# Four GNN layers on one core: 46 instead of 29 bundles of edges counted in the first layer, and their turned products five tiles later

## The reference, cut to what matters

```python
def setup_inputs(seed=0):
    x   # 6250 x 128, float32
    src = randint(0, 6250)                    # 200000
    dst = (6250 * uniform ** 2.0)             # 200000, then both sorted by dst
    edge_type_8, edge_weight1                 # 8 relations, one weight per edge

def reference(...):
    h = relu(layernorm(x)); x = x + layer1(h, src, dst)   # mean of h[src] over the edges of a node, W, b
    h = relu(layernorm(x)); x = x + layer2(h, src, dst)   # gates:
        theta = h[dst] - h[src]
        w = sigmoid(relu(theta @ W1 + b1) @ W2 + b2)
        agg = segment_sum(w * theta, dst) + indeg * (h @ W4 + b4)
    h = relu(layernorm(x)); x = x + layer3(h, src, dst)   # mean of relu(h @ Wp.T + bp)[src]
    h = relu(layernorm(x)); x = x + layer4(h, src, dst)   # sum over 8 relations, weight per edge
    return x
```

## Time and profile before

| | |
|---|---|
| time, median of 3 runs | 6365.12 us (6364.78 to 6367.93) |
| span of the profiled execution | 6426.8 us |
| layer 1, edges | 107 to 1233 us |
| layer 2, edges | 1304 to 3642 us |
| layer 3, edges | 3700 to 4320 us |
| layer 4, edges | 4530 to 6426 us |
| busy over the span | PE 60%, DVE 46%, ACT 22%, POOL 62% |
| indirect DMAs | 3505 on GpSimd |
| stores of counts | 29 in layer 1, 19 in layer 2 |

### The profile page before, as it was taken

One profiled execution on the slowest core, in us unless ns is written; L12 is line 12 of the kernel. 1 busy time (PEld: TensorE's weight loads), 2 busy tenths in 40 slices (PEclk: granted clock), 3 DMA queues, 4 the chain that ended last, 5 costly groups with the idle time before them and its releaser, 6 DMA issues.

```text
span 6426.8 us, 68888 instructions
## 1 busy us (share of the span) xinstructions
PE 3872.2 (60%) x20122; PEld 2959.4 (46%) x20154; DVE 2933.5 (46%) x9989; ACT 1413.8 (22%) x5474; POOL 3972.3 (62%) x4198
## 2 busy tenths in 40 slices
PE   4676766655555565555555578876565565665433
PEld 3333434445544454455455456653344444444332
DVE  7555544556555565556555633342333222222222
ACT  4222122333333333333333401121000000000000
POOL 4556666456666666666666466646566666666665
PEclk7778778777777777777777789998777777777666
DMA  3333333345455454544545455555211111111121
GB/s 107 96 101 110 111 105 116 107 140 155 143 150 148 147 150 144 154 145 141 159 144 151 123 184 198 195 181 178 69 46 46 45 47 45 46 45 46 46 61 46
DMA packets 323521, 734.49 MB, mean 114 GB/s; under 512 B 77056, under 2 KB 164124, under 8 KB 310860
## 3 DMA queue, kind: packets, MB, share of 16 engines
q0 software_dynamic: 172432, 405.32, 23.2%
q1 hardware_dynamic: 148700, 323.81, 14.9%
q10 hardware_dynamic: 2016, 0.92, 0.1%
HBM read 598.71 MB, written 131.05 MB: 114 GB/s over the span
## 4 chain that ended last, share of the span: by engine, by line
another core or an unknown queue 30%; PE 27%; DVE 19%; issue 15%; ACT 4%; DMA 2%; DVEq 1%; SPq 1%; ACTq 0%
PE ps L2574 8%; DVE oneh L1863 6%; PE ps L2559 3%; PE ps L2530 3%; PE ps L2537 2%; DVE ps L1998 2%; PE ps L2469 2%; PE ps L2597 2%; DMA third<-dst_flat 2%; ACT turned_words L1681 1%; DVE third L1990 1%; PE ps L2419 1%; DVE turned_words L1955 1%; DVE tmp L1954 1%
## 5 line engine op out<-in xcount | busy, mean ns | idle before, releaser
L1470 POOL DMA_INDIRECT rows<-tab_rel,third x1299 | 1247.0, 960 | 646.9 <-issue 367.1
L1470 POOL DMA_INDIRECT rows<-tab_h,idx_src x1086 | 1046.7, 964 | 723.4 <-issue 345.8
L1470 POOL DMA_INDIRECT rows<-tab_hp,idx_src x1120 | 1077.1, 962 | 622.5 <-issue 298.8
L2597 PE MATMUL ps<-third 128*128 128x128 f32 x3126 | 607.1, 353 | 501.6 <-issue 295.8
L2530 PE MATMUL ps<-oneh,rows 128*128 128x128 f32 x2598 | 489.1, 340 | 607.1 <-DVE oneh L1863 330.7
L2597 PEld LDWEIGHTS ps<-third 128*128 128x128 f32 x3126 | 539.6, 258 | 593.7 <-issue 355.3
L2574 PE MATMUL ps<-third,h 128*120 128x384 bf16 (+17 forms) x3773 | 715.0, 337 | 65.8 <-issue 34.6
L2530 PEld LDWEIGHTS ps<-oneh,rows 128*128 128x128 f32 x2598 | 432.6, 245 | 695.8 <-DVE oneh L1863 362.6
L1681 ACT ACTIVATE turned_words<-turned_words 128x128 f32<-128x128 f32 x1563 | 463.1, 300 | 690.8 <-DVE turned_words L2003 527.5
L2574 PEld LDWEIGHTS ps<-third,h 128*120 128x120 bf16 (+10 forms) x3773 | 487.8, 133 | 239.4 <-issue 61.3
L1470 POOL DMA_INDIRECT third<-tab_hp,idx_src x443 | 425.9, 961 | 231.7 <-issue 118.5
(11 more groups left out here) (279 smaller groups left out, 5495.4 us busy)
## 6 DMA issues: line engine op xcount, KB each, us to landing
third<-dst_flat SPq DMA_DIRECT2D x390, 256.0 KB
h<-cnt_d SPq DMA_DIRECT2D x48, 1568.0 KB
cnt_d<-h SPq DMA_DIRECT2D x29, 1568.0 KB
cnt_d<-third SPq DMA_DIRECT2D x19, 1568.0 KB
tab_rel<-third SPq DMA_DIRECT2D x49, 512.0 KB
rows<-tab_rel,third POOLq DMA_INDIRECT x1299
rows<-tab_hp,idx_src POOLq DMA_INDIRECT x1120
rows<-tab_h,idx_src POOLq DMA_INDIRECT x1086
```

The lines of the kernel that those rows point to most:

```text
L1470: pool.indirect_dma_start(out=to[:, t, 0:n], out_offset=None, in_=table[:, :], in_offset=bass.IndirectOffsetOnAxis(ap=idx[:, col:col + 1], ...
L2597: last = pe.matmul(ps_t[sl][:, t * P:(t + 1) * P], onehT[:, sl, t * P:(t + 1) * P], pwin[:, st["v"] % 2, :], start=True, stop=True)
```

## The change

Three numbers are changed or added. `FIRST_SHARE` goes from 880/1563 to 1160/1563. With it 46 bundles (1148 tiles) are counted in layer 1 and 415 tiles (104 groups) gathered there, and 2 bundles (20 tiles) are left for layer 2. The 17 bundles that move have windows of 14 to 17 columns and 14 to 18 tiles each. `per_turn` of layer 1 goes from 2346.8 to 6205.8 ns, that of layer 2 from 262.7 to 19.7 ns. `LATE_TURN` and `LATE_ADD` put the turned product of a bundle in layer 1 five steps (before one) behind `pack_out`, and the addition three steps (before one) behind the turned product. Layer 3 keeps its steps and its work. Nothing else differs. The changed lines of the constants and of `multiply` move later code down by one and by three lines (L2559 is L2562 after it, L2584 is L2587).

```diff
@@ -25,7 +25,8 @@
 PACK = 2
 PACK_SHARE = 1168 / 1563
 
-FIRST_SHARE = 880 / 1563
+FIRST_SHARE = 1160 / 1563
+LATE_TURN, LATE_ADD = 5, 3
 BUNDLE = 128
 
 PACKS3 = ((4, 36), (2, 76), (1, 148))
@@ -885,10 +886,12 @@
                     plan.append(("pack_mm", dict(st, q0=q0, q1=min(nb, q0 + MULTIPLY_STEP))))
                     yield MULTIPLY_STEP * H3 / 2.4
                 plan.append(("pack_out", st))
-                yield 0.0
+                for _ in range(LATE_TURN if layer == 0 else 1):
+                    yield 0.0
                 st["added"] = n_added.get(u - 1, 0)
                 plan.append(("pack_turn", st))
-                yield 0.0
+                for _ in range(LATE_ADD if layer == 0 else 1):
+                    yield 0.0
                 plan.append(("pack_add", dict(u=u, sums=sums, turn=n_turn[u], add=s_add.value)))
                 n_added[u] = s_add.up()
                 yield 0.0
```

## The result

The changed kernel takes 6218.91 us (median of 4 runs, 6206.78 to 6221.39) against 6366.52 us (6364.78 to 6371.44): a ratio of 0.9767, 95% interval 0.9749 to 0.9785. The forecast was 6307 us. The direction was right and the time lies in the range, but the gain is 148 us where 58 were forecast. And it is a gain only on some chips: the runs further down fell on several chips, of two kinds, and on the second kind, where the kernel before takes 5463 us, the same change makes it 1.5% slower.

The account below looks back on a forecast made before the run. Layer 1 was taken as bound by a chain, not an engine, with TensorE waiting before the turned product. Layer 1 +26 us (610 less 46 x 12.7) and layer 2 -84 gave -58: 6365.1 to 6307 us, 8-in-10 range 6170 to 6520.

Parts of the forecast that it names:

- Seventeen more bundles: Layer 1: 17 more bundles, each costing what a late bundle cost before, 35.9 us: +610 us.
- Fewer gathered groups: Layer 1: 3.7 fewer groups a bundle, 1.3 us of TensorE scatter each: 4.8 us saved a bundle.
- The late turned product: Layer 1: counts fill TensorE's wait before the turned product, 6.9 us saved a bundle, ends 1.7 and 13.8.
- Rival A: End of each layer 1 product: signals stay late, only 8.3 us saved a bundle, 6509 us, slower; chance 0.33.
- The moved addition: Layer 1: covered by the counting, 0.34 us on VectorE needed only 16 tiles later: nothing gained.
- Signals that come sooner: Layer 1 products: fewer groups between steps and a higher clock, 1 us saved a bundle, ends 0 and 16.
- Stores: Layer 1: seventeen stores of 1568 KB move in, DMA share 0.35, SyncE otherwise free there: nothing.
- Layer 2: Layer 2 without 276 late tiles: faster gathers and fewer waits for loads behind stores, -84 us.
- rival C: Layer 2 gives nothing, gathers keep 1.46 to 1.50 us each; only +26 us left, 6391 us; chance 0.08.
- The sum: Whole kernel: layer 1 +26 us, layer 2 -84, layers 3 and 4 0: -58 us, median 6307 us.
- Rival B: Layer 1: pause goes and clock stays high, 20.4 us a bundle, layer 1 -103, total 6178 us; chance 0.14.

Follow-up runs that it names:

- The share alone: Against the kernel before, 46 bundles counted in layer 1, turned product and addition one step behind as before: ratio 0.9812 on the first kind, 1.0209 on the second.
- 34 and 38 bundles: Kernel before with that many bundles in layer 1, turned product 5 and addition 3 steps behind: 6311.92 and 6258.05 us first kind, 5413.01 and 5461.14 us second.
- the late steps alone: Kernel before, 29 bundles kept, only turned product 5 and addition 3 steps behind: 6358.37 us, ratio 0.9986 on the first kind, 0.9988 on the second.

## Why the prediction was right in direction and wrong in size

*Seventeen more bundles, +610 us at 35.9 each.* As a price of the late bundles of before it was right. But it already held the cost of the gathers beside a bundle, and that was not the TensorE time that I subtracted.

*Fewer gathered groups, 4.8 us a bundle (3.7 groups at 1.3 us).* This is the step that failed. The share alone took a bundle from 35.9 to 19.4 us late in layer 1, 16.5 us for 3.7 groups, 4.5 us a group. I had priced a group by its scatter on TensorE, 0.8 to 1.6 us, and given its gathers nothing, since GpSimd waits for TensorE in the earlier trace rows. The run with half of the gathers on the first kind shows the opposite: with half of the gathers gone and all scatters left, the layer is 745 us, about 300 us shorter. A sign was there. By the plan a late bundle had 24 gathers in 35.9 us, 1.50 us each, like layer 2; counted in the trace it is 44 gathers in the 71.8 us between three stores, 1.63 us each. Such near rates in stages with other work point to what they have in common, but they don't give the price: the rate is no constant, as 34 and 38 bundles showed.

*The late turned product, 6.9 us a bundle.* This failed too. It is worth 0.7 us: 31 us over 46 bundles with the share (998 to 967 on the same chip), late addition included; alone, over 29 bundles, it is 20 us against the long first profile and 10 us, not clear of none, in the time. Rival A described this step as it happened: TensorE got no pair, and its wait for pairs rose from 37.1 to 169.2 us. I had its row, the eviction that began 1.7 us before the turned product, and took the mean wait nevertheless. Even the low end, 1.7 us, was too much. The term was also more than its own filling: five tiles of 0.61 us are 3.1 us of work for TensorE, and four were moved (six for two), so it could not have covered 6.9 us on average.

*The moved addition, nothing.* On the second kind it seems to be worth 14 us, 0.3 us a bundle, half of what the late steps bring there. It was not run by itself on the first.

*Signals that come sooner, 1 us a bundle.* The ends were 0 and 16 and I took the wrong one. This is where the time came from: from a product's first matmul to its copy 21.3 us on average before, 12.2 after. It overlaps with the term of the groups, as both are the gathers' doing. Saved were 17.4 us a bundle late in the layer (35.9 to 18.5: 16.5 by the share, 0.9 by the late steps), forecast 12.7. Over the whole layer it was less, (610 + 99)/46 = 15.4 us. That the total came within 5 us a bundle is luck: 6.0 us too much for the turned product stood against 10.7 us too little for the gathers (groups and signals together, 16.5 for 5.8).

*Stores, nothing.* No run takes them alone. Nothing waits for them in the rows shown, and on the second kind the same 17 more stores stand in a layer in which TensorE is busy for 874 of 1015 us.

*Layer 2, -84 us.* Too much. It is 69 us less between the profiles of before and after, but only 36 against the profile of the late steps alone, whose layer 2 is the code of before (2310 and 2274 us). With 34 and with 38 bundles it is 2286 us, so it does fall with the late tiles. On the second kind it is nothing (1984 and 1982 us), as rival C had it: there GpSimd bounds it at 1.27 us a gather.

*The sum.* Layer 1 was to become 26 us longer and became 99 us shorter by the profiles. The spans of these two differ by 208 us, 60 more than the times, since the first one is long. Two profiles of one chip close better, the late steps alone and the change: 80 us in layer 1, 36 in layer 2 and 7 in an earlier start of the first product are 123 of the 128 us between their spans. So most of the gain is in layer 1, where the forecast had a loss.

*Rival B* (0.14) came nearest for layer 1: -103 us at 20.4 us a bundle. Its ground was wrong, as the share brought it and not the covered pause. On the clock it was right: 0.92 where it was 0.76. The Trainium skill (TensorE: Matmul & The Clock Gate, Part 1, "HAM oscillation") says that a gap in TensorE's work, repeated in each round, makes each round start at the low clock. The trace agrees: with the pauses gone a counted tile takes 0.47 us in place of 0.61. Whether the single records of the clock can be trusted was not tested. With half of the gathers TensorE did the same products in the same order and the copy came 1.1 us after the last matmul, so the pause doesn't belong to these products by themselves.

*What stays open.* Why the signals of TensorE come late beside dense gathers on one kind of chip and not on the other wasn't settled. The runs show that it follows the gathers and grows with their number, and that half of them leave nothing of it; they don't show what the gathers and the signals share, nor whether GpSimd's work or the traffic of the rows does it, since each run changed both. A late signal also can't be told here from a TensorE that is slowed beside the gathers and whose matmuls are recorded as ended too early. The forecast treated the chip of the first profile as the chip, and nothing that it read there told of another kind on which the sign is the other.

## What to carry to other kernels

Before a piece of work is priced by one engine's part in it, take only that part away in a run: here half of the scatters gone saved nothing (second kind) and half of the gathers gone saved some 120 us of the layer (second kind) and 300 us (first kind), while the forecast had priced the scatters alone. The time of a stage over the number of its transfers is a hint to look there. On the second kind it named the bound (1.26 to 1.27 us in layers 2 and 4, and 1.25 in a bundle); on the first kind a price made of it missed layer 1 by over 100 us, 905 for 1027. A wait's mean is no price for covering it: count first the work that is moved into it. A wait that ends with many others at once isn't taken away by moving the instruction that shows it; look at what was released 1 to 2 us earlier. And a balance between engines should be timed on more than one chip before it is moved far: here 17 bundles more are 2.3% faster on one kind and 1.5% slower on another, while 5 bundles more are 0.8% and 1.0% faster (all with the late steps).

## What the runs showed of the hardware

- Two kinds of chips. The unchanged kernel takes 6365 to 6369 us (medians, two chips at least) on one and 5463 to 5467 us (three chips) on the other. Layer 4's 1299 gathers start 1.45 and 1.26 us apart on average, with 944 ns for each on both. The median distance is 1.25 us on both; distances of more than 2 us are 81 of 1298 on the first kind and none on the second.
- On the first kind ScalarE's copy of a product starts up to 14 us after the recorded end of TensorE's last matmul of it when gathers run densely beside (7.8 us on average with 24 gathers in a bundle), and 1.0 us after it with 9 gathers in a bundle of half the length. On the second kind it is 1.3 us with all gathers.
- With 346 gathers in layer 1 the two kinds agree within a microsecond (745 and 744 us).
- The profiles of the second kind show at most a few us of waits for "remote". On the first kind they all do in layer 2, and in layer 1 only with 38 bundles or fewer and all of their gathers.
